# First turned weight tile of a two-layer LoRA kernel: loaded on ScalarE's queue, laid in two PSUM banks, copied by two engines

## The chip, the cores and the metric

The kernel runs on 1 core of one Trainium2 chip. The metric is device time in microseconds (us), the median of several runs. Engines are named as in the profile: PE is TensorE (PEld its weight loads), DVE is VectorE, ACT is ScalarE, POOL is GpSimd, SP is SyncE, which issues the transfers.

## The reference, cut to what matters

```python
# x: (8, 256, 1024) float32; W0, W1: (1024, 1024); ranks 32 and 16
def layer0(x, label, W, lora_A, lora_B_w):          # scale 0.5
    return x @ W.T + (x @ lora_A[label]) @ lora_B_w.T * 0.5
def layer1(x, slot, W, b, lora_As, lora_Bs):        # scale 2
    return x @ W.T + b + (x @ lora_As[slot]) @ lora_Bs[slot] * 2
x = x + layer0(x, itok_B_0_2, ...)                  # the label is chosen per batch
x = x + layer1(x, itok_B_0_23, ...)                 # and so is the slot
```

## The kernel before, in words

With the identity added to both weight matrices, the two layers are one product of x with V = (I + W0 transposed)(I + W1 transposed), and a low-rank part for each batch. The kernel first computes V once (up to about 89 us of the span), then goes over the 8 batches, each in some 22.6 us. Both products use a scheme of seven products of 512 x 512 quarters instead of eight. Every float32 operand is split in a high part (`_hi`, rounded to the matmul's format) and a low part (`_lo`, the rest); each product is hi x hi + hi x lo + lo x hi.

The order of the work is written out by hand for each engine; engines wait for each other by semaphores.

What matters here is the start, quarter (1,1) of both matrices: `a11` (of W0, loaded as it lies by `load_a`, 2 KB rows) and `b11` (of W1, which must be transposed first). Each comes in 4 tiles j = 0 to 3 of 256 KB. A tile of W1 is loaded to `n11` by `load_n` (in pieces of 512 bytes), the identity is added to its diagonal block (`n_eyed`; DVE does tile 0, POOL the others), PE transposes its four 128 x 128 blocks into one PSUM bank (`turn_b11`, semaphore `turned`), ACT copies the bank to `b11_hi` (`b11_high`, `w1_hi_made`), DVE computes `b11_lo` = bank - `b11_hi` (`b11_low`, `w1_lo_made`), and ACT copies the bank once more to `b11` (`b11_copy`, `w1_made`). For `a11`, DVE (tiles 0 and 1) casts to `a11_hi` (`w0_hi_made`); of tile 0 it casts columns 256 to 511 first, then adds the identity and casts columns 0 to 255.

PE starts with 14 matmuls on constants (`warm_up(14)`, 256 columns of bfloat16, whose result nothing reads), then transposes tile 0, issues 5 more such matmuls (`warm_up(5)`), and goes on with `vm1_high(0)`: 4 matmuls `a11_hi` x `b11_hi` (which wait for `w1_hi_made` and `w0_hi_made`), 4 with `b11_lo` (which wait for `w1_lo_made`), then the transposes of tile 1, and so on.

SP issues all transfers, in the order n11 tile 0, a11 tile 0, n11 tile 1, a11 tile 1, ... In the profile's rows `n`, `a`, `b_hi`, `a_hi`, `b_lo`, `a_lo`, `b` are these tiles with their numbers left out; `n_68` is n11, `a_49` is a11 and `b_52` is b11 in the listings of instructions.

Of the kernel before, what the change touches and what calls it, by code (L numbers as in the profile page):

```python
# [20 lines left out]
def two_layer_lora_kernel(nc, x, label0, slot1, w0, a0, b0w, w1, bias, a1, b1, out):  # L21
# [130 lines left out]
    with ExitStack() as ctx:  # L152
        bank = [ctx.enter_context(nc.psum_tensor(f"bank{n}", [P, 512], F32)) for n in range(8)]

        def sem(name):
            return ctx.enter_context(nc.semaphore(name))
# [64 lines left out]
        corr_done, h_made, u_hi_made, u_lo_made = sem("corr_done"), sem("h_made"), sem("u_hi_made"), sem("u_lo_made")  # L221
        e_st_made, m2_done = sem("e_st_made"), sem("m2_done")
        u0_hi_made, u0_lo_made = sem("u0_hi_made"), sem("u0_lo_made")
        m1_done, m6_done, m5_done, m7_done = sem("m1_done"), sem("m6_done"), sem("m5_done"), sem("m7_done")
        m1_made, u2_made, z_made, z2_made = sem("m1_made"), sem("u2_made"), sem("z_made"), sem("z2_made")
# [26 lines left out]
        def quarter(t, g):  # L252
            return t[:, HK * (g % 2):HK * (g % 2) + HK, P * (g // 2):P * (g // 2) + P]

        def last_half(h):
            dst = out[B - 1, :, sides[h]].rearrange("(p odd) i -> odd p i", odd=2)
            return dst[0], y[:, C11, sides[h]]
# [6 lines left out]
        def _(sp):  # L264
            w0_v = w0.rearrange("(b j p) (a i) -> p b j a i", b=2, p=P, a=2)
            w1_v = w1.rearrange("(n t p) (b j k) -> p n t b j k", n=2, p=P, b=2, k=P)

# [198 lines left out]
        def _(act):  # L466
# [188 lines left out]
            def batch(b, first, final):  # L655
# [60 lines left out]
        def _(dve):  # L716
# [23 lines left out]
            def b11_low(j):  # L740
                dve.wait_ge(w1_hi_made, j + 1)
                tt(b11_lo[:, j, :], TURN_BANK[j][:, :], b11_hi[:, j, :].bitcast(F32), ALU.subtract, w1_lo_made)
# [9 lines left out]
            def a11_high(j, cols):  # L752
                nc.vector.tensor_copy(a11_hi[:, j, cols], a11[:, j, cols]).then_inc(w0_hi_made, 1)

            for j in range(2):
                dve.wait_ge(a11_in[j], 16)
                if j == 0:
                    a11_high(0, sides[1])
                part = a11[:, j, P * j:P * j + P]
                tt(part, part, eye[:, :], ALU.add, w0_eyed)  # L760
                dve.wait_ge(w0_eyed, j + 1)
                a11_high(j, slice(0, H) if j else sides[0])
                b11_low(j)
                a11_low(j)
# [14 lines left out]
            def t1_sum(j):  # L779
                dve.wait_ge(w1_made, j + 1)  # L780
                tt(t1[:, j, :], TURN_BANK[T12_AT[j]][:, :], b11[:, j, :], ALU.subtract, t1_made)

            def t3_sum(j):
                dve.wait_ge(turned, T12_AT[j] + 1)
                dve.wait_ge(w1_made, HK + j + 1)
                tt(t3[:, j, :], TURN_BANK[T12_AT[j]][:, :], b22[:, j, :], ALU.subtract, t3_made)
# [63 lines left out]
            def b22_low(h):  # L850
                dve.wait_ge(w1_hi_made, 2 * HK + h + 1)
                dve.wait_ge(t2_made, h + 1)
                low(b22_lo, b22, b22_hi, PAIR[h], w1_lo_made)
# [7 lines left out]
            def t4_sum(h):  # L861

                dve.wait_ge(t2_made, h + 1)
                dve.wait_ge(w1_made, 2 * HK + 2 * h + 2)
                tt(t4[:, PAIR[h], :], b21[:, PAIR[h], :], t2[:, PAIR[h], :], ALU.subtract, t4_made)
# [32 lines left out]
            def b21_low(j):  # L898
                dve.wait_ge(w1_made, 2 * HK + j + 1)
                tt(b21_lo[:, j, :], TURN_BANK[T21_AT[j]][:, :], b21_hi[:, j, :].bitcast(F32), ALU.subtract, w1_lo_made)  # L900
# [205 lines left out]
            def batch(b, first, final):  # L1106
# [27 lines left out]
                def z_second():  # L1134
                    dve.wait_ge(m7_done, b + 1)
                    dve.wait_ge(z_made, b + 1)
                    tt(z_sum[:, :], BANK_D[:, :], z_sum[:, :], ALU.add, z2_made)
# [64 lines left out]
        def _(pe):  # L1202
# [8 lines left out]
            def row_tile(tile, j, m):  # L1211
                return tile[:, j, P * m:P * m + P]


            taken = ([(w1_made, j + 1) for j in range(HK)] + [(w1_made, HK + 1), (w1_made, HK + 2)]
                     + [(t1_made, 1), (t1_made, 2)] + [(w1_made, HK + 3), (w1_made, HK + 4)]
                     + [(t1_made, 3), (t1_made, 4)] + [(w1_lo_made, HK + 1)])

# [45 lines left out]
            def vm1_high(j):  # L1264

                pe.wait_ge(w1_hi_made, j + 1)
# [7 lines left out]
                pe.wait_ge(w1_lo_made, j + 1)  # L1274
                for m in range(HK):
                    mm(LOW[m][:, :], row_tile(a11_hi, j, m), b11_lo[:, j, :], False, False)
# [32 lines left out]
            pe.wait_ge(eye_steps, 2)  # L1309
            turn_b11(0)  # L1310
            warm_up(5)
# [47 lines left out]
            for j in range(HK):  # L1359
                pe.wait_ge(w1_lo_made, HK + j + 1)  # L1360
# [3 lines left out]
            pe.wait_ge(w1_made, 3 * HK)  # L1364
            c_first(0, A11)
# [6 lines left out]
            for j in range(HK):  # L1372
                q_step(Q_BANK[1], j, T3, j, j == 0, False)
            pe.wait_ge(w1_lo_made, 2 * HK + 2)
            for j in range(HK):
# [96 lines left out]
            def of(hi, lo):  # L1472
                return lambda k: (hi[:, k, :], lo[:, k, :])

            def batch(b, first, final):
# [33 lines left out]
                else:  # L1509
                    pe.wait_ge(c_made[C21], b)  # L1510
                product(BANK_D, s_of(3), of(vt3_hi, vt3_lo), True, m7_done)
                if not first:
# [14 lines left out]
                if not final:  # L1527
                    product(BANK_A, *second, False, m2_done, corrects=True)
# [70 lines left out]
```

## Time and profile before

| | |
|---|---|
| median of 3 runs | 294.64 us (294.39 to 294.78) |
| the profiled execution: its own time | 294.97 us |
| its span (first to last instruction) | 293.2 us |
| PE busy | 289.5 us (99%) |
| DVE / ACT / POOL busy | 242.9 / 153.6 / 31.3 us |

The span is shorter than the time of the same execution by 1.8 us, which lies around the kernel. The profile's busy time counts a matmul until its modelled end, so matmuls that follow each other overlap in the rows; how fast PE works is read from the distance of their starts.

### The profile page before, as it was taken

The page shows a single profiled execution, that of the slowest core. Times are in us where ns is not written, and L with a number is a line of the kernel's source. Part 1 is how long each engine was busy: PE and PEld are TensorE (multiplying, and loading weights), DVE is VectorE, ACT ScalarE, POOL GpSimd, SP SyncE. Part 2 cuts the span into 40 slices and gives each one's busy share as a digit, 9 for nine tenths or more (in the row PEclk, how much of TensorE's full clock was granted, in tenths as well). Part 3 has the DMA queues.
Part 4 walks back from the last instruction along what each step waited for, and adds up shares of the span by engine and source line. Part 5 has one row for each costly group of instructions (what it writes and reads, how often), then busy time and mean ns, then how long its engine had stood idle before and what let it go on. Part 6 is the DMA issues. An engine that isn't in the chain of part 4 may idle for free.

```text
span 293.2 us, 4450 instructions
## 1 busy us (share of the span) xinstructions
PE 289.5 (99%) x1337; PEld 236.1 (81%) x1337; DVE 242.9 (83%) x368; ACT 153.6 (52%) x270; POOL 31.3 (11%) x81
## 2 busy tenths in 40 slices
PE   8999999999999999999999999999999999999996
PEld 6888888888888888878878878878878878878875
DVE  3779998999999999999996897797798698695432
ACT  3574677879257637464453463373364355355120
POOL 0716500010000501000100100100100100100000
PEclk9999999999999999999999999999999999999999
DMA  6999530800006610074277077068068059013004
GB/s 200 315 275 345 79 43 6 141 1 2 0 0 110 97 28 1 6 125 157 46 117 199 22 120 198 18 101 221 6 108 212 15 101 233 6 36 144 0 1 145
DMA packets 100803, 29.17 MB, mean 99 GB/s; under 512 B 85548, under 2 KB 93996, under 8 KB 100788
## 3 DMA queue, kind: packets, MB, share of 16 engines
q1 hardware_dynamic: 100788, 28.99, 42.4%
q8 instruction: 7, 0.11, 0.2%
q14 instruction: 8, 0.07, 0.1%
HBM read 20.59 MB, written 8.39 MB: 99 GB/s over the span
## 4 chain that ended last, share of the span: by engine, by line
PE 99%; DVE 0%; issue 0%
PE bank L1204 95%; PE bank L1228 3%; PE bank L1449 1%; PE bank L1416 0%; DVE y L718 0%
## 5 line engine op out<-in xcount | busy, mean ns | idle before, releaser
L1204 PE MATMUL bank<-v_hi,lhs 128*128 128x512 f32 (+1 forms) x136 | 42.6, 378 | 0.0
L1204 PE MATMUL bank<-vt_lo,s_hi 128*128 128x512 f32 x96 | 37.4, 389 | 0.0
L1204 PE MATMUL bank<-vt_hi,s_hi 128*128 128x512 f32 x96 | 37.4, 389 | 0.0
L1204 PE MATMUL bank<-vt_hi,s_lo 128*128 128x512 f32 x96 | 37.4, 389 | 0.0
L969 DVE STREAM_TRANSPOSE xt<-raw 128x512 int32<-128x512 int32 x32 | 32.5, 1076 | 0.5 <-DMA raw<-in_x 0.4
L1204 PEld LDWEIGHTS bank<-v_hi,lhs 128*128 128x128 f32 x136 | 25.1, 188 | 4.8
L468 ACT ACTIVATE lhs<-xt 128x512 fp32r<-128x512 f32 x32 | 19.6, 626 | 13.0 <-PE bank L1204 12.7
L1204 PE MATMUL bank<-v_lo,lhs 128*128 128x512 f32 (+1 forms) x68 | 25.9, 380 | 0.0
L1204 PE MATMUL bank<-vt_hi,lhs 128*128 128x512 f32 x64 | 22.1, 406 | 0.0
L718 DVE TENSOR_TENSOR lhs<-xt,lhs 128x512 fp32r<-128x512 f32 x32 | 21.7, 687 | 0.3
L434 POOL CAST ac<-c_hi 128x128 fp32r (+1 forms) x16 | 7.1, 446 | 135.7 <-PE bank L1204 98.6
L718 DVE TENSOR_TENSOR s_lo<-s_sum,s_hi 128x512 fp32r<-128x512 f32 x32 | 21.2, 686 | 0.2 <-ACT s_hi L468 0.2
L1204 PEld LDWEIGHTS bank<-vt_lo,s_hi 128*128 128x128 f32 x96 | 18.0, 188 | 3.7
L1204 PEld LDWEIGHTS bank<-vt_hi,s_hi 128*128 128x128 f32 x96 | 18.0, 188 | 3.7
L1204 PEld LDWEIGHTS bank<-vt_hi,s_lo 128*128 128x128 f32 x96 | 18.0, 188 | 3.7
L468 ACT ACTIVATE s_hi<-s_sum 128x512 fp32r<-128x512 f32 x32 | 19.1, 624 | 2.1 <-DVE s_sum L718 1.8
L1204 PE MATMUL bank<-t_hi,s_hi 128*128 128x512 f32 x48 | 19.1, 397 | 0.0
L1204 PE MATMUL bank<-t_hi,s_lo 128*128 128x512 f32 x48 | 18.8, 391 | 0.0
L1204 PE MATMUL bank<-t_lo,s_hi 128*128 128x512 f32 x48 | 18.7, 390 | 0.0
L468 ACT ACTIVATE u_part<-bank 64x256 f32<-64x256 f32 x8 | 3.1, 381 | 28.0 <-PE bank L1204 28.0
L718 DVE TENSOR_TENSOR y<-bank,u_sum 128x512 f32<-128x512 f32 x16 | 11.0, 687 | 6.6 <-PE bank L1204 6.6
L468 ACT ACTIVATE vt_hi<-vt 128x512 fp32r<-128x512 f32 x16 | 10.1, 631 | 11.0 <-DVE vt L718 10.5
(167 smaller groups left out, 665.1 us busy)
## 6 DMA issues: line engine op xcount, KB each, us to landing
raw<-in_x SPq DMA_DIRECT2D x32, 256.0 KB, 4.8
out<-y SPq DMA_DIRECT2D x31, 256.0 KB, 2.7
n<-in_L_cond_W SPq DMA_DIRECT2D x16, 256.0 KB, 5.6
a<-in_L_cond_W SPq DMA_DIRECT2D x16, 256.0 KB, 5.6
a_raw<-in_L_cond_lora_A SPq DMA_DIRECT2D x8, 128.0 KB, 2.4
b_raw<-in_L_cond_lora_Bs SPq DMA_DIRECT2D x16, 64.0 KB, 2.2
e_raw<-in_L_cond_lora_Bs SPq DMA_DIRECT2D x32, 32.0 KB, 1.8
a_raw<-in_L_cond_lora_As SPq DMA_DIRECT2D x8, 64.0 KB, 2.6
```

Of the source, the lines that this page charges most:

```text
L434: nc.gpsimd.tensor_copy(ac[:, :, at_col:at_col + R1], c_hi[:, :, cols].bitcast(F32)).then_inc(ac_c_made, 1)
L468: nc.scalar.activation(out_ap, in_ap, COPY, scale=scale).then_inc(made, 1)
L718: nc.vector.tensor_tensor(out_ap, one, other, op).then_inc(made, 1)
L969: nc.vector.transpose(xt[:, n, :, :].rearrange("p e (s sb) -> p sb e s", sb=GR).bitcast(I32), rows[:, n // 2, n % 2].bitcast(I32)).then_in ...
L1204: return nc.tensor.matmul(ps, lhsT, rhs, start=start, stop=stop, skip_group_check=more)
L1228: last = nc.tensor.transpose(ps[:, P * t:P * t + P], tile[:, j, t, :], eye[:, :])
L1449: return nc.tensor.matmul(ps, e_st[rows, P * t:P * t + P], e_p[rows, cols], start=False, stop=True, skip_group_check=True, tile_position=( ...
```

## The change

Five edits.

1. n11 tile 0 is issued by ACT, as its first instruction, in place of SP. SP's list begins with a11 tile 0.
2. The four transposes of tile 0 go to two banks: blocks 2 and 3 to bank 4 (the bank of tile 2), blocks 1 and 0 to bank 6, in the order 2, 3, 1, 0. After block 3 a new semaphore `half_turned` is raised, after block 0 `turned` as before.
3. DVE casts columns 256 to 511 of `b11_hi` tile 0 from bank 4 after `half_turned`; ACT copies columns 0 to 255 from bank 6 after `turned`.
4. `b11_lo` and `b11` of tile 0 are made in two halves each (2 x 256 columns in place of 512), one for each bank.
5. The counts of `w1_hi_made`, `w1_lo_made` and `w1_made` are one higher from there on. `m2_done` and `m7_done` of the batches become one semaphore `m72_done`, raised twice per batch (odd counts in place of `m7_done`, even ones of `m2_done`). The transposes of tile 2 now wait for the copies of tile 0.

```diff
         TURN_BANK = [bank[n] for n in (6, 7, 4, 5, 6, 7, 4, 5, 6, 7, 4, 6, 7, 4, 6, 7)]
-        TURNED_THERE = {4: 0, 5: 1, 6: 2, 7: 3, 8: 4, 9: 5, 10: 6, 11: 8, 12: 9, 13: 10, 14: 11, 15: 12}
+        TURNED_THERE = {2: 0, 4: 0, 5: 1, 6: 2, 7: 3, 8: 4, 9: 5, 10: 6, 11: 8, 12: 9, 13: 10, 14: 11, 15: 12}
+        FIRST_BANK = [TURN_BANK[0], TURN_BANK[2]]
...
             for j in range(HK):
-                load_n(n11, 0, 0, j, n11_in[j])
+
+                if j > 0:
+                    load_n(n11, 0, 0, j, n11_in[j])
                 load_a(a11, 0, 0, j, a11_in[j])
...
             def b11_copy(j):
-                act.wait_ge(w1_lo_made, j + 1)
+                act.wait_ge(w1_lo_made, j + 2)
                 bank_copy(b11, j, TURN_BANK[j], w1_made)
 
-            for j in range(2):
-                b11_high(j)
-                b11_copy(j)
+            act.dma_start(n11[:, 0, :, :], w1_v[:, 0, :, 0, 0, :]).then_inc(n11_in[0], 16)
+            act.wait_ge(turned, 1)
+            copy(b11_hi[:, 0, sides[0]], FIRST_BANK[0][:, sides[0]], w1_hi_made)
+            for h in range(2):
+                act.wait_ge(w1_lo_made, h + 1)
+                copy(b11[:, 0, sides[h]], FIRST_BANK[h][:, sides[h]], w1_made)
+            b11_high(1)
+            b11_copy(1)
...
                 if not final:
-                    act.wait_ge(m2_done, b + 1)
+                    act.wait_ge(m72_done, 2 * b + 2)
                     a_high(b + 1, 1)
...
-                    act.wait_ge(m7_done, b + 1)
+                    act.wait_ge(m72_done, 2 * b + 1)
...
+            dve.wait_ge(half_turned, 1)
+            nc.vector.tensor_copy(b11_hi[:, 0, sides[1]], FIRST_BANK[1][:, sides[1]]).then_inc(w1_hi_made, 1)
             for j in range(2):
                 dve.wait_ge(a11_in[j], 16)
...
-                b11_low(j)
+                if j == 0:
+                    dve.wait_ge(w1_hi_made, 2)
+                    for h in range(2):
+                        tt(b11_lo[:, 0, sides[h]], FIRST_BANK[h][:, sides[h]], b11_hi[:, 0, sides[h]].bitcast(F32),
+                           ALU.subtract, w1_lo_made)
+                else:
+                    b11_low(j)
                 a11_low(j)
...
             warm_up(14)
             pe.wait_ge(eye_steps, 2)
-            turn_b11(0)
+
+            pe.wait_ge(n11_in[0], 16)
+            for t in (2, 3, 1, 0):
+                if t == 0:
+                    pe.wait_ge(n_eyed, 1)
+                last = nc.tensor.transpose(FIRST_BANK[t // 2][:, P * t:P * t + P], n11[:, 0, t, :], eye[:, :])
+                if t == 3:
+                    last.then_inc(half_turned, 1)
+            last.then_inc(turned, 1)
             warm_up(5)
             vm1_high(0)
             turn_b11(1)
```

ACT's first instructions, before the change (names as above; `turned` and the like are the semaphores that an instruction waits for):

```order
L465 UNCONDITIONAL_BRANCH [waits barrier_Pool_Activation_PE_DVE_SP_release]
L468 ACT_TABLE_LOAD
L468 ACTIVATE b_hi<-bank 128x512 [waits turned]
L468 ACTIVATE b_52<-bank 128x512 [waits w1_lo_made]
L468 ACTIVATE b_hi<-bank 128x512 [waits turned]
```

and the same place of the changed kernel:

```order
L470 UNCONDITIONAL_BRANCH [waits barrier_Pool_Activation_PE_DVE_SP_release]
L496 DMA n_68<-in_L_cond_W 128x4x128
L473 ACT_TABLE_LOAD
L473 ACTIVATE b_hi<-bank 128x256 [waits turned]
L473 ACTIVATE b_52<-bank 128x256 [waits w1_lo_made] x2
L473 ACTIVATE b_hi<-bank 128x512 [waits turned]
```

The transfer stands ahead of the table load, and the first two copies have become one of 256 columns and two of 256.

DVE's first instructions, before the change:

```order
L718 TENSOR_TENSOR n_68<-n_68,eye 128x128 [waits n11_in0,eye_steps]
L753 CAST a_hi<-a_49 128x256 [waits a11_in0]
L718 TENSOR_TENSOR a_49<-a_49,eye 128x128
L753 CAST a_hi<-a_49 128x256 [waits w0_eyed]
L718 TENSOR_TENSOR b_lo<-bank,b_hi 128x512 [waits w1_hi_made]
L718 TENSOR_TENSOR a_lo<-a_49,a_hi 128x512 [waits w0_hi_made]
```

and of the changed kernel:

```order
L728 TENSOR_TENSOR n_68<-n_68,eye 128x128 [waits n11_in0,eye_steps]
L766 CAST b_hi<-bank 128x256 [waits half_turned]
L763 CAST a_hi<-a_49 128x256 [waits a11_in0]
L728 TENSOR_TENSOR a_49<-a_49,eye 128x128
L763 CAST a_hi<-a_49 128x256 [waits w0_eyed]
L728 TENSOR_TENSOR b_lo<-bank,b_hi 128x256 [waits w1_hi_made]
L728 TENSOR_TENSOR b_lo<-bank,b_hi 128x256
L728 TENSOR_TENSOR a_lo<-a_49,a_hi 128x512 [waits w0_hi_made]
```

A cast from PSUM has come in ahead of the casts of a11, and the subtraction for `b_lo` is two. PE executes the same instructions as before in the same order; only the blocks and banks of its first four transposes differ.

## Rows read from the trace of the kernel before

**Rows 1.** The page: busy times, the chain that ended last.

```profile
span 293.2 us, 4450 instructions
PE 289.5 (99%) x1337; PEld 236.1 (81%) x1337; DVE 242.9 (83%) x368; ACT 153.6 (52%) x270; POOL 31.3 (11%) x81
...
PE 99%; DVE 0%; issue 0%
```

**Rows 2.** Windows: PE, PEld, DVE, ACT, POOL busy (count), PEclk, DMA share, GB/s.

```profile
9.16:24.00 14.84, 14.84 (x88) 12.79 (x87) 12.81 (x23) 10.44 (x19) 5.80 (x12) 1.00 1.02 299
24.00:60.00 36.00, 36.00 (x172) 30.09 (x171) 34.01 (x39) 24.96 (x36) 9.47 (x12) 1.00 0.54 104
60.00:285.00 225.00, 225.00 (x1010) 182.38 (x1009) 190.41 (x297) 115.14 (x213) 14.59 (x52) 1.00 0.36 79
```

**Rows 3.** Timeline from the start: start us, length us, engine, instruction.

```profile
0.78 0.45 SPq L272 DMA_DIRECT2D n<-in_L_cond_W  x1
0.79 1.28 ACT L468 ACT_TABLE_LOAD   x1 [0.79 <-PEq L1588]
...
0.83 3.15 PE L1204 MATMUL bank<-const-bfloat16-1.0 128*128 128x256 bf16 x14 [0.83 <-PEq L1588]
...
1.29 0.49 SPq L269 DMA_DIRECT2D a<-in_L_cond_W  x1
...
3.97 0.29 DVE L718 TENSOR_TENSOR n<-n,eye 128x128 f32<-128x128 f32 x1 [3.97 <-DMA n<-in_L_cond_W]
4.00 1.09 PE L1228 MATMUL bank<-eye,n 128*128 128x128 f32 x4
4.88 1.27 PE L1204 MATMUL bank<-const-bfloat16-1.0 128*128 128x256 bf16 x5
5.07 0.29 DVE L753 CAST a_hi<-a 128x256 fp32r<-128x256 f32 x1 [0.81 <-DMA a<-in_L_cond_W]
5.13 0.60 ACT L468 ACTIVATE b_hi<-bank 128x512 fp32r<-128x512 f32 x1 [3.06 <-PE bank L1228]
5.28 0.28 DVE L718 TENSOR_TENSOR a<-a,eye 128x128 f32<-128x128 f32 x1
...
5.59 0.29 DVE L753 CAST a_hi<-a 128x256 fp32r<-128x256 f32 x1
...
5.81 0.68 DVE L718 TENSOR_TENSOR b_lo<-bank,b_hi 128x512 fp32r<-128x512 f32 x1
...
6.41 0.68 DVE L718 TENSOR_TENSOR a_lo<-a,a_hi 128x512 fp32r<-128x512 f32 x1
6.75 0.87 PEld L1204 LDWEIGHTS bank<-b_lo,a_hi 128*128 128x128 f32 x4
6.97 1.07 PE L1204 MATMUL bank<-b_lo,a_hi 128*128 128x512 f32 x4
...
8.51 0.60 ACT L468 ACTIVATE b_hi<-bank 128x512 fp32r<-128x512 f32 x1 [1.39 <-PE bank L1228]
```

**Rows 4.** Timeline of the window 6.0 to 6.3: what runs in it.

```profile
5.74 0.42 PE L1204 MATMUL bank<-const-bfloat16-1.0 128*128 128x256 bf16 x1
5.78 0.69 PEld L1204 LDWEIGHTS bank<-b_hi,a_hi 128*128 128x128 f32 x3
...
5.81 0.86 PE L1204 MATMUL bank<-b_hi,a_hi 128*128 128x512 f32 x2
```

**Rows 5.** Tile views of n, then of a: time from issue to landing.

```profile
DMA to landing us min/median/max: 3.1/5.6/8.0
...
DMA to landing us min/median/max: 3.8/5.5/7.2
```

**Rows 6.** Page, costliest groups: xcount, busy us, mean ns, idle us before.

```profile
L1204 PE MATMUL bank<-vt_lo,s_hi 128*128 128x512 f32 x96 | 37.4, 389 | 0.0
...
L468 ACT ACTIVATE lhs<-xt 128x512 fp32r<-128x512 f32 x32 | 19.6, 626 | 13.0 <-PE bank L1204 12.7
...
L468 ACT ACTIVATE u_part<-bank 64x256 f32<-64x256 f32 x8 | 3.1, 381 | 28.0 <-PE bank L1204 28.0
```

More of the change, by code:

```diff
@@ L221, in two_layer_lora_kernel @@
         corr_done, h_made, u_hi_made, u_lo_made = sem("corr_done"), sem("h_made"), sem("u_hi_made"), sem("u_lo_made")
-        e_st_made, m2_done = sem("e_st_made"), sem("m2_done")
+        e_st_made, half_turned = sem("e_st_made"), sem("half_turned")
         u0_hi_made, u0_lo_made = sem("u0_hi_made"), sem("u0_lo_made")
-        m1_done, m6_done, m5_done, m7_done = sem("m1_done"), sem("m6_done"), sem("m5_done"), sem("m7_done")
+        m1_done, m6_done, m5_done, m72_done = sem("m1_done"), sem("m6_done"), sem("m5_done"), sem("m72_done")
         m1_made, u2_made, z_made, z2_made = sem("m1_made"), sem("u2_made"), sem("z_made"), sem("z2_made")
@@ L253, in quarter @@
             return t[:, HK * (g % 2):HK * (g % 2) + HK, P * (g // 2):P * (g // 2) + P]
+        w1_v = w1.rearrange("(n t p) (b j k) -> p n t b j k", n=2, p=P, b=2, k=P)
         def last_half(h):
@@ L265, in _ @@
             w0_v = w0.rearrange("(b j p) (a i) -> p b j a i", b=2, p=P, a=2)
-            w1_v = w1.rearrange("(n t p) (b j k) -> p n t b j k", n=2, p=P, b=2, k=P)
             def load_a(tile, a, b, j, there):
@@ L740, in b11_low @@
             def b11_low(j):
-                dve.wait_ge(w1_hi_made, j + 1)
+                dve.wait_ge(w1_hi_made, j + 2)
                 tt(b11_lo[:, j, :], TURN_BANK[j][:, :], b11_hi[:, j, :].bitcast(F32), ALU.subtract, w1_lo_made)
@@ L779, in t1_sum @@
             def t1_sum(j):
-                dve.wait_ge(w1_made, j + 1)
+                dve.wait_ge(w1_made, j + 2)
                 tt(t1[:, j, :], TURN_BANK[T12_AT[j]][:, :], b11[:, j, :], ALU.subtract, t1_made)
@@ L784, in t3_sum @@
                 dve.wait_ge(turned, T12_AT[j] + 1)
-                dve.wait_ge(w1_made, HK + j + 1)
+                dve.wait_ge(w1_made, HK + j + 2)
                 tt(t3[:, j, :], TURN_BANK[T12_AT[j]][:, :], b22[:, j, :], ALU.subtract, t3_made)
@@ L850, in b22_low @@
             def b22_low(h):
-                dve.wait_ge(w1_hi_made, 2 * HK + h + 1)
+                dve.wait_ge(w1_hi_made, 2 * HK + h + 2)
                 dve.wait_ge(t2_made, h + 1)
@@ L863, in t4_sum @@
                 dve.wait_ge(t2_made, h + 1)
-                dve.wait_ge(w1_made, 2 * HK + 2 * h + 2)
+                dve.wait_ge(w1_made, 2 * HK + 2 * h + 3)
                 tt(t4[:, PAIR[h], :], b21[:, PAIR[h], :], t2[:, PAIR[h], :], ALU.subtract, t4_made)
@@ L898, in b21_low @@
             def b21_low(j):
-                dve.wait_ge(w1_made, 2 * HK + j + 1)
+                dve.wait_ge(w1_made, 2 * HK + j + 2)
                 tt(b21_lo[:, j, :], TURN_BANK[T21_AT[j]][:, :], b21_hi[:, j, :].bitcast(F32), ALU.subtract, w1_lo_made)
@@ L1134, in z_second @@
                 def z_second():
-                    dve.wait_ge(m7_done, b + 1)
+                    dve.wait_ge(m72_done, 2 * b + 1)
                     dve.wait_ge(z_made, b + 1)
@@ L1212, in row_tile @@
                 return tile[:, j, P * m:P * m + P]
-            taken = ([(w1_made, j + 1) for j in range(HK)] + [(w1_made, HK + 1), (w1_made, HK + 2)]
-                     + [(t1_made, 1), (t1_made, 2)] + [(w1_made, HK + 3), (w1_made, HK + 4)]
-                     + [(t1_made, 3), (t1_made, 4)] + [(w1_lo_made, HK + 1)])
+            taken = ([(w1_made, j + 2) for j in range(HK)] + [(w1_made, HK + 2), (w1_made, HK + 3)]
+                     + [(t1_made, 1), (t1_made, 2)] + [(w1_made, HK + 4), (w1_made, HK + 5)]
+                     + [(t1_made, 3), (t1_made, 4)] + [(w1_lo_made, HK + 2)])
             def turn(tile, j, n, eyed=0):
@@ L1264, in vm1_high @@
             def vm1_high(j):
-                pe.wait_ge(w1_hi_made, j + 1)
+                pe.wait_ge(w1_hi_made, j + 2)
                 if j > 0:
@@ L1273, in vm1_high @@
                     mm(LOW[m][:, :], row_tile(a11_hi, j, m), b11_hi[:, j, :], j == 0, False)
-                pe.wait_ge(w1_lo_made, j + 1)
+                pe.wait_ge(w1_lo_made, j + 2)
                 for m in range(HK):
@@ L1359, in _ @@
             for j in range(HK):
-                pe.wait_ge(w1_lo_made, HK + j + 1)
+                pe.wait_ge(w1_lo_made, HK + j + 2)
                 last = q_step(Q_BANK[0], HK + j, B21, j, False, j == HK - 1)
@@ L1363, in _ @@
             pe.wait_ge(a1_lo_made, 1)
-            pe.wait_ge(w1_made, 3 * HK)
+            pe.wait_ge(w1_made, 3 * HK + 1)
             c_first(0, A11)
@@ L1373, in _ @@
                 q_step(Q_BANK[1], j, T3, j, j == 0, False)
-            pe.wait_ge(w1_lo_made, 2 * HK + 2)
+            pe.wait_ge(w1_lo_made, 2 * HK + 3)
             for j in range(HK):
@@ L1510, in batch @@
                     pe.wait_ge(c_made[C21], b)
-                product(BANK_D, s_of(3), of(vt3_hi, vt3_lo), True, m7_done)
+                product(BANK_D, s_of(3), of(vt3_hi, vt3_lo), True, m72_done)
                 if not first:
@@ L1527, in batch @@
                 if not final:
-                    product(BANK_A, *second, False, m2_done, corrects=True)
+                    product(BANK_A, *second, False, m72_done, corrects=True)
                     h_ready()
```

## The prediction

> **What bounds the kernel now.** I read the page first: PE is busy 289.5 of 293.2 us and the chain that ended last is PE alone for 99% of the span [rows 1]. The windows say where the rest is: from 9.16 us to 285 us PE is busy in every hundredth of a us [rows 2]. So nothing after the first ten microseconds waits for data, and whatever the change does there must show as a shift of everything behind: the kernel ends earlier or later by as much as PE's first real matmuls do, and by nothing else. The timeline of the start is the place to read [rows 3].
>
> There PE does this. It works on constants from 0.83 us; n11 tile 0 has landed when DVE and PE go on at 3.97 and 4.00; four transposes; five matmuls on constants; then the first matmul of the product at 5.81 [rows 4], those with b_lo at 6.97 [rows 3]. Two candidates could hold that 5.81. One is the copy of ACT, 5.13 to 5.73, with the weight load at 5.78 [rows 3, 4]. The other is PE itself. The 14 matmuls on constants take 3.15 us with the last one 0.42 long: 2.73 over 13 distances, 0.21 us for 256 columns, which is 1.2 GHz, the lower level of the clock. The last of the five starts at 5.74 [rows 4], so its columns occupy the array until 5.74 + 0.21 = 5.95. The first real matmul then has to fall in from 5.95, whatever its row says as a start. The second real one agrees: two of them take 0.86 us from 5.81 [rows 4], and one at full clock is 0.39 long [rows 6], so it starts at 6.28. That is 0.33 behind 5.95, midway between 0.43 (512 columns at 1.2 GHz) and 0.23 (the distance at 2.4 GHz, (1.07 - 0.39) / 3 [rows 3, 6]). So half of its columns ran at either level, and the clock rose near 6.15. The clock column of the windows shows 1.00 throughout and doesn't tell this; the distances do.
>
> So both are nearly tied: ACT's copy lets the array start near 5.95 too (weight load at 5.78, and some 0.1 to 0.2 until its matmul runs), and the five matmuls on constants end there. The start of the transposes, which is the landing of n11 tile 0, sets both: 4.00 plus 9 distances of 0.21 is 5.92, plus a rest of 0.03.
>
> **The change part by part.**
>
> *Half copies of b11_hi.* ACT copied 512 columns in 0.60 us [rows 3]; a copy of 256 columns took 0.38 [rows 6]. It ends 0.22 earlier, at 5.51 instead of 5.73 if the landing is the same. DVE's cast from the other bank can start when the second transpose is through, 0.7 us behind the start of the first (0.21 distance, 0.42 length, a wait's 0.04), at T + 0.7, where T is the start of the transposes. I take 0.3 for it (256 columns from SBUF took 0.29 [rows 3]; this one reads PSUM, which no row has for a cast; the far bound is half of the 0.68 subtraction and a fixed part, 0.45). It ends by T + 1.15 at the latest, ahead of ACT. So b11_hi is ready 0.22 earlier. What this gives on PE is at most 0.03, since the matmuls on constants stand until T + 1.95 while the clock is at the lower level. The gain of 0.22 is covered; it would be had in full only if the clock rose before the transposes.
>
> *b_lo.* DVE's row is now: cast b_hi, cast a_hi, add, cast a_hi, two halves of b_lo. With distances from the rows (5.07 to 5.28 to 5.59 to 5.81: 0.21, 0.31, 0.22; a 512-column subtraction frees DVE after 0.60, 5.81 to 6.41; half of it about 0.33) b_lo is complete at T + 0.71 + 0.24 + 0.74 + 0.33 + 0.41 = T + 2.43; before it was 6.49 = T + 2.49 [rows 3]. The additional cast is paid by the fact that a11 no longer is waited for: the cast of a_hi began at 5.07 because a11 landed then. Equal, so no gain, and no loss as long as a11 is there by T + 0.95.
>
> *The second copy, b11, in halves.* 2 x 0.38 in place of 0.60 on ACT, which next has work when tile 1 is turned, at 8.51 [rows 3]. Covered.
>
> *The semaphore `m72_done`.* The counts keep the same two waits. In the loop over batches ACT gets two more register instructions per round; ACT waits 12.7 us in all in front of one group of copies there and PE is busy all through [rows 2, 6]. Zero.
>
> *The transfers.* This is the term that decides. Before, SP issued n11 tile 0 at 0.78 and a11 tile 0 at 1.29 [rows 3]; they landed 3.1 and 3.8 later, 3.9 and 5.1 [rows 3, 5]. ACT left the same barrier at 0.79 [rows 3], so n11 tile 0 is issued no earlier than before. What changes is the company: a11 tile 0 is issued at 0.78 too, on the other queue, and takes part in the same 16 DMA engines from the beginning instead of half a microsecond later and behind. a11 and all that SP issues behind it go 0.5 us earlier; n11 tile 0, on which everything hangs, can only lose. Bounds: nothing lost (landing 3.9, T = 4.00), and a11's bytes wholly ahead (n11 lands last, at the old 5.0 to 5.1 of a11, T = 5.1). A tile of 256 KB takes 0.87 us at the 299 GB/s of a stretch in which the DMA engines are busy throughout [rows 2]; of a11's 0.87 us the part counts that is moved in front of n11's last pieces. With two queues served in turn I take half of it, 0.45: T = 4.45.
>
> [...]
>
> *What 0.45 later costs PE.* Until 6.15 the array works at half speed, so a delay there is partly paid back: fewer columns run at 1.2 GHz. From T = 4.45 eight of the nine distances pass by 6.15 (1.70 us), the ninth at 2.4 GHz takes 0.11: 6.26. The first real matmul takes 0.23 more; the second runs from 6.49 where it was 6.28. That is +0.21. b_lo is ready at 4.45 + 2.43 = 6.88, its weight load would stand at about 6.95: just not late. Behind it the order on PE is unchanged, and SP's transfers come earlier, so the shift stays +0.21 to the end.
>
> **Sum.** 0.21 from the landing, -0.03 to 0 from the half copies, 0 from the others: about +0.2 us. Against the profiled execution that is 294.97 + 0.2 = 295.2; that execution lies 0.33 above the median, and I give the median: 294.64 + 0.2 = 294.8. A measurement of this kernel tells about 0.2% (0.6 us) from no change, so the forecast is "no difference".
>
> **The rivals.**
>
> *a11 goes ahead of n11 (slower).* With T = 5.1, ACT's half copy ends at 5.1 + 1.09 + 0.04 + 0.38 = 6.6, b_lo at 5.1 + 2.43 = 7.5, and the matmuls with b_lo start at 7.75 (0.22 behind their weight load) instead of 6.97: +0.8 us, 295.4. [...] Against: n11's issue takes less time (0.45 against 0.49), so it is not behind. Chance 0.12. Above T = 4.85 it decides at the 0.6 us bound.
>
> *The clock rises later (slower).* The clock rose at 6.15 after work with one break of 0.2 us before 4.00. At T = 4.45 the break is 0.7 us. If it puts off the rise, each us of that costs half a us of matmuls at 1.2 GHz; I price a rise at 9.2, three groups of matmuls and one of transposes later: 3.0 / 2 = 1.5 us, 296.1. For it: the order of events alone; one rise is all that the trace shows. [...] Against: the break stays short beside the work around it. Chance 0.07.
>
> *No contention (slightly faster).* n11 lands as before or, alone in its queue, a little earlier. PE could start at 3.77, when its last warm-up leaves the array (it starts at 3.98 - 0.42 = 3.56 and needs 0.21). Then nine distances end at 5.7, the first real matmul runs mostly at 1.2 GHz and is through at about 6.12, the second at 6.35 instead of 6.51: -0.16 us, 294.5. Even this is within 0.2%. A gain of 0.6 us has no place in the rows: b_lo at T + 2.43 would allow at most 0.3. Chance 0.2, and 0.05 beyond for a faster result that I can't name.
>
> **How the numbers follow.** The forecast (+0.0 to +0.6) has 0.56, no contention 0.20, a11 ahead 0.12, the clock 0.07, unnamed gain 0.05. Of a11 ahead about two thirds lie over 0.6 us. Faster by over 0.2%: 0.05; slower: 0.08 + 0.07, 0.15; within: 0.80. The range goes from no contention with the spread of the runs (-0.25) to 294.2, and up to a11 ahead, 295.4; the late clock and a small rest are left out.
>
> **What would show it.** n11's transfer on ACT's queue and DVE's add of the identity later than 3.97, near 4.4; the cast of b_hi by DVE 0.7 behind the first transpose; ACT's copy of 256 columns about 0.38; a11's cast waiting for no DMA; the second real matmul near 6.5; PE busy from there as before. Wrong if DVE's add stands at 3.97 or earlier while the time falls by 0.6 (then ACT's copy was the bound after all), or if matmuls of 512 columns keep the long form beyond 6.5 (the clock).

## The result: 0.6% slower

The changed kernel takes 296.89 us (median of 9 runs, 296.00 to 297.46) against 294.92 us for the kernel before (9 runs, 294.39 to 295.89). The medians are 1.97 us apart. The ratio is 1.0063, with a 95% interval from 1.0052 to 1.0074, which is 1.9 us (1.5 to 2.2): slower by 0.6%, where "no difference" was forecast. The range, 294.2 to 295.4, doesn't hold it. The profiled execution took 297.46 us with a span of 295.7, 2.5 us more than the span of before, so it is one of the longer ones.

The timeline of the changed kernel's start (start us, length us, engine, instruction; ACTq and SPq are issues of transfers):

```profile
0.78 0.40 SPq L272 DMA_DIRECT2D a<-in_L_cond_W  x1
0.78 0.47 ACTq L496 DMA_DIRECT2D n<-in_L_cond_W  x1
...
0.83 3.15 PE L1222 MATMUL bank<-const-bfloat16-1.0 128*128 128x256 bf16 x14 [0.83 <-PEq L1614]
...
5.34 0.29 DVE L728 TENSOR_TENSOR n<-n,eye 128x128 f32<-128x128 f32 x1 [5.34 <-DMA n<-in_L_cond_W]
...
5.38 1.09 PE L1333 MATMUL bank<-eye,n 128*128 128x128 f32 x4 [1.40 <-DMA n<-in_L_cond_W]
...
6.08 0.42 DVE L766 CAST b_hi<-bank 128x256 fp32r<-128x256 f32 x1 [0.44 <-PE bank L1333]
...
6.42 0.35 DVE L763 CAST a_hi<-a 128x256 fp32r<-128x256 f32 x1
6.50 0.38 ACT L473 ACTIVATE b_hi<-bank 128x256 fp32r<-128x256 f32 x1 [3.93 <-PE bank L1333]
...
7.18 2.06 PE L1222 MATMUL bank<-b_hi,a_hi 128*128 128x512 f32 x4
7.21 0.74 DVE L728 TENSOR_TENSOR b_lo<-bank,b_hi 128x256 fp32r<-128x256 f32 x2
...
9.04 1.51 PE L1222 MATMUL bank<-b_lo,a_hi 128*128 128x512 f32 x4
...
11.02 0.60 ACT L473 ACTIVATE b_hi<-bank 128x512 fp32r<-128x512 f32 x1 [2.65 <-PE bank L1246]
```

Two things have happened. First, n11 tile 0 landed 1.37 us later: DVE's add stands at 5.34 where it stood at 3.97 [rows 3]. PE's row of the transposes says that it was idle for 1.40 us before them, waiting for this transfer. Second, the matmuls behind run longer than before. Taken one by one in the trace, the four with b_hi start at 7.18, 7.76, 8.18 and 8.61 and the first three with b_lo at 9.04, 9.46 and 9.89: from the second one on they are 0.43 apart, the pace of the matmuls on constants in front of them (256 columns every 0.213 us), where in the kernel before they were 0.23 apart from the second one on. Only the last distance, 9.89 to 10.16, is shorter, so the clock rose near 10 us. The trace says the same: beside the instructions it has entries of the granted clock, and the first of them, a share of 1.00, begins at 9.94 us here and at 6.15 in the kernel before. The four with b_lo begin 2.07 late (9.04 against 6.97), and ACT's copy of tile 1 is 2.51 late (11.02 against 8.51). The spans differ by 2.5, so that is the whole difference, and the windows say that nothing is added behind it (busy us of PE, PEld, DVE, ACT, POOL, clock, DMA share, GB/s):

```profile
5.00:24.00 19.00, 18.62 (x96) 15.64 (x97) 15.23 (x31) 10.63 (x20) 8.29 (x14) 1.00 1.13 325
24.00:285.00 261.00, 261.00 (x1181) 212.72 (x1180) 225.71 (x335) 140.88 (x250) 20.41 (x62) 1.00 0.38 81
```

PE is busy 261.00 of 261.00 us, as in [rows 2]; its only idle time behind 5.00 is the 0.38 us in front of the transposes. The chain of waits of the changed kernel has the transfer in it, 2% of the span, which it had not before [rows 1]:

```profile
PE 97%; DMA 2%; DVE 0%; issue 0%
PE bank L1222 93%; PE bank L1246 2%; DMA n<-in_L_cond_W 2%; PE bank L1475 1%; PE bank L1333 0%; PE bank L1442 0%; DVE y L728 0%
```

### The profile page after: what moved, and what is told of

The parts are those of the page before. It is cut to its first block, busy times and chain, and to the rows that moved or that the text cites. A ratio compares the mean times of both kernels' runs of the same rounds, so it can differ in the third digit from the quotient of the medians.

```text
span 295.7 us, 4466 instructions
## 1 busy us (share of the span) xinstructions
PE 290.6 (98%) x1337; PEld 236.9 (80%) x1337; DVE 243.8 (82%) x370; ACT 153.6 (52%) x271; POOL 29.4 (10%) x81
## 4 chain that ended last, share of the span: by engine, by line
PE 97%; DMA 2%; DVE 0%; issue 0%
PE bank L1222 93%; PE bank L1246 2%; DMA n<-in_L_cond_W 2%; PE bank L1475 1%; PE bank L1333 0%; PE bank L1442 0%; DVE y L728 0%
## 5 line engine op out<-in xcount | busy, mean ns | idle before, releaser
L1222 PE MATMUL bank<-lhs,ac 128*128 128x512 f32 x64 | 15.8, 389 | 0.0
```

What stands on the lines that cost most here:

```text
L1222: return nc.tensor.matmul(ps, lhsT, rhs, start=start, stop=stop, skip_group_check=more)
```

## The experiments

All times are medians, each against runs of the kernel before made beside it. Of each kernel one execution was profiled; of the others only the times are known. The questions: is it the queue or the half copies; why does n11 come so late; and what does the clock add?

### The queue alone, the half copies alone

First the queue alone, on the kernel before:

```diff
+            act.dma_start(n11[:, 0, :, :], w1_v[:, 0, :, 0, 0, :]).then_inc(n11_in[0], 16)
             for j in range(2):
                 b11_high(j)
...
-                load_n(n11, 0, 0, j, n11_in[j])
+                if j > 0:
+                    load_n(n11, 0, 0, j, n11_in[j])
```

> The kernel before, with nothing changed but that n11 tile 0 is issued by ScalarE in place of SyncE. Theory 1 (the two queues share the DMA engines, and the late landing moves all that follows): n11 tile 0 lands at about 5.3 us as in the changed kernel (before: 3.9), and the time is 2 to 2.5 us above the kernel before. Theory 2 (the late landing or the loss comes from the half copies and their waits): landing at 3.9 and no loss.

296.80 us against 295.05, ratio 1.0052 (1.0035 to 1.0070). The transfer landed at 5.26. The loss is there without one half copy, and with 5 runs it can't be told from that of the whole change (1.0052 to 1.0074).

Then the changed kernel with the transfer back on SyncE:

```diff
-            act.dma_start(n11[:, 0, :, :], w1_v[:, 0, :, 0, 0, :]).then_inc(n11_in[0], 16)
...
-                if j > 0:
-                    load_n(n11, 0, 0, j, n11_in[j])
+                load_n(n11, 0, 0, j, n11_in[j])
```

> The changed kernel with n11 tile 0 issued by SyncE first, as before; the two banks, the half copies and the merged semaphore stay. Theory 1: landing at 3.9 again, b_hi ready at 5.5 instead of 5.73, hidden behind the matmuls on constants: within 0.3 us of the kernel before. Theory 2 (half copies cost): 1 to 2.5 us slower. Theory 3 (the clock hides nothing): 0.2 us faster.

295.09 us against 295.05, ratio 1.0004 (0.9995 to 1.0013). With the landing in time, the two banks, the half copies and the merged semaphore neither cost nor give anything that can be measured. The timeline of this run shows how the shorter copy is lost:

```profile
4.29 1.08 PE L1330 MATMUL bank<-eye,n 128*128 128x128 f32 x4 [0.32 <-DMA n<-in_L_cond_W]
5.17 1.27 PE L1219 MATMUL bank<-const-bfloat16-1.0 128*128 128x256 bf16 x5
...
5.41 0.38 ACT L471 ACTIVATE b_hi<-bank 128x256 fp32r<-128x256 f32 x1 [3.35 <-PE bank L1330]
...
6.10 1.29 PE L1219 MATMUL bank<-b_hi,a_hi 128*128 128x512 f32 x4
```

ACT was through at 5.79, but the real matmuls start at 6.10, 1.81 behind the transposes, as before (4.00 and 5.81): the matmuls on constants fill that time. The landing was 0.3 later in this execution (4.26 against 3.97), though SyncE's list was that of the kernel before; this much it varies by itself.

### Why n11 is late: which transfer goes first

Queue for queue, the transfers of the changed kernel from 1.8 to 2.8 us and, behind the "...", from 2.8 to 3.8 (packets, MB, share of the 16 engines). q1 is SyncE's queue, q10 ScalarE's:

```profile
q1 hardware_dynamic: 79, 0.16, 75.1%
...
q10 hardware_dynamic: 259, 0.13, 44.6%
q1 hardware_dynamic: 61, 0.10, 41.0%
```

In the first microsecond in which bytes move, ScalarE's queue moves nothing at all. The 79 packets carry 0.16 MB, 2 KB each: rows of a11. It isn't a sharing in turn, as I had assumed. Either ScalarE's queue starts late in itself, or something lets a11 pass first. The next kernels tell these apart. Each is the kernel before with one tile, or half of one, issued by ScalarE; their diffs leave out lines already shown.

With the queues changed about (a11 on ScalarE, n11 first on SyncE):

```diff
+            act.dma_start(a11[:, 0, :], w0_v[:, 0, 0, 0, :]).then_inc(a11_in[0], 16)
...
-                load_a(a11, 0, 0, j, a11_in[j])
+                if j > 0:
+                    load_a(a11, 0, 0, j, a11_in[j])
```

> The kernel before with a11 tile 0 issued by ScalarE at 0.8 us and n11 tile 0 still first on SyncE. Two transfers start together as in the changed kernel, with the queues changed about. Theory A (the engines serve the two queues in turn, and the tile in 512-byte pieces loses): n11 tile 0 lands late again, 4.6 to 5.3 us. Theory B (a transfer issued by ScalarE starts behind the one that SyncE issued, whatever it holds): n11 tile 0 lands near 3.9 as before and a11 tile 0 is the late one, 5.0 or later. Time: A 1 to 2 us slower, B within 0.6 us.

296.18 us against 295.07, ratio 1.0042 (1.0024 to 1.0059). Its queues in the same two stretches:

```profile
q10 hardware_dynamic: 72, 0.15, 57.5%
...
q1 hardware_dynamic: 294, 0.15, 50.4%
q10 hardware_dynamic: 69, 0.11, 35.3%
```

Now SyncE's queue is the one that moves nothing for a microsecond, and n11 on it landed at 5.16. Theory B, by which ScalarE's transfer stands behind, is refuted; the landing is as theory A said, but not for its reason. The ten times lie in two groups, five from 295.57 to 295.64 and five from 296.71 to 297.55; the section on the clock comes back to them. The timeline from 0.7 to 1.2 us gives the two issues:

```profile
0.78 0.46 SPq L273 DMA_DIRECT2D n<-in_L_cond_W  x1
0.79 0.42 ACTq L493 DMA_DIRECT2D a<-in_L_cond_W  x1
```

a11's issue ended at 1.21 and n11's at 1.24; in the changed kernel they ended at 1.18 and 1.25, and in the kernel with the queue alone at 1.18 and 1.26. Each time a11's ended first, and a11 went first.

With ScalarE's transfer alone (n11 on ScalarE, and SyncE waiting for its landing):

```diff
+            sp.wait_ge(n11_in[0], 16)
             for j in range(HK):
```

> n11 tile 0 issued by ScalarE at 0.8 us, and SyncE issues nothing before it has landed. For its landing only: everything behind is late and the time says nothing. Theory B1 (a transfer on ScalarE's queue starts a microsecond late in itself): landing at 4.8 or later though nothing else moves. Theory B2 (it starts late because SyncE's transfer is prepared first): landing at 3.9.

The landing, by DVE's add:

```profile
0.78 0.43 ACTq L494 DMA_DIRECT2D n<-in_L_cond_W  x1
...
3.73 0.29 DVE L722 TENSOR_TENSOR n<-n,eye 128x128 f32<-128x128 f32 x1 [3.73 <-DMA n<-in_L_cond_W]
```

Landed by 3.73: the queue isn't slow. (Its time, 297.79 us from one run, says nothing here, for its other loads wait.)

With n11 on ScalarE again and SyncE's a11 put back to about where it was in time (1.49, before the change 1.29), behind the two small index loads:

```diff
+            sp.dma_start(index[0:1, 0:B], label0.rearrange("(o b) -> o b", o=1)).then_inc(index_in, 16)
+            sp.dma_start(index[0:1, B:2 * B], slot1.rearrange("(o b) -> o b", o=1)).then_inc(index_in, 16)
             for j in range(HK):
...
-                if j == 2:
-                    sp.dma_start(index[0:1, 0:B], label0.rearrange("(o b) -> o b", o=1)).then_inc(index_in, 16)
-                    sp.dma_start(index[0:1, B:2 * B], slot1.rearrange("(o b) -> o b", o=1)).then_inc(index_in, 16)
```

> n11 tile 0 issued by ScalarE at 0.8 us; SyncE issues the two small index transfers first and then a11 tile 0 at about 1.4 us, where it stood before the change. Theory B2 (who is first is prepared first): n11 tile 0 lands near 3.9 to 4.2 and the time is within 0.6 us of the kernel before. Theory A (served in turn): landing at 4.5 or later. Theory B1 (ScalarE's queue starts late in itself): 4.9 or later, 1 to 2.5 us slower.

294.88 us against 295.07, ratio 0.9990 (0.9978 to 1.0002). The loss is gone:

```profile
0.79 0.43 ACTq L492 DMA_DIRECT2D n<-in_L_cond_W  x1
...
1.49 0.36 SPq L270 DMA_DIRECT2D a<-in_L_cond_W  x1
...
3.75 0.29 DVE L720 TENSOR_TENSOR n<-n,eye 128x128 f32<-128x128 f32 x1 [3.75 <-DMA n<-in_L_cond_W]
...
4.51 0.29 DVE L755 CAST a_hi<-a 128x256 fp32r<-128x256 f32 x1 [0.47 <-DMA a<-in_L_cond_W]
```

Its queues from 1.8 to 2.8 us: only ScalarE's moves, now 400 packets of n11.

```profile
q10 hardware_dynamic: 400, 0.20, 69.1%
```

With one index load instead of two ahead of it, so that a11's issue starts 0.3 us earlier:

```diff
+            sp.dma_start(index[0:1, 0:B], label0.rearrange("(o b) -> o b", o=1)).then_inc(index_in, 16)
             for j in range(HK):
```

> The kernel before; ScalarE issues n11 tile 0, SyncE issues one small index transfer and then a11 tile 0, at about 1.2 us, so that its issue ends 0.3 us behind that of n11 (in the changed kernel it ended 0.07 us ahead). Theory B2 (whoever has issued first is prepared first, whatever it holds): n11 lands at 3.6 to 3.9 and a11 by 4.5; time within 0.4 us of the kernel before. Rival (the tile in 2 KB rows goes ahead of the one in 512-byte pieces when both are near in time): n11 at 4.5 or later, 1 us slower or more.

295.19 us against 294.97, ratio 1.0001 (0.9991 to 1.0012).

```profile
0.79 0.43 ACTq L493 DMA_DIRECT2D n<-in_L_cond_W  x1
1.21 0.37 SPq L270 DMA_DIRECT2D a<-in_L_cond_W  x1
...
3.87 0.29 DVE L721 TENSOR_TENSOR n<-n,eye 128x128 f32<-128x128 f32 x1 [3.87 <-DMA n<-in_L_cond_W]
```

n11's issue ended at 1.22 and a11's at 1.58, and n11 went first. And the mirror, on the kernel before: ScalarE issues the two index loads and then a11, SyncE n11 first.

> The kernel before; ScalarE issues the two index transfers and then a11 tile 0, at about 1.5 us; SyncE issues n11 tile 0 first. The mirror of the run in which ScalarE had n11 and SyncE came later. If only the order in time counts and not the queue: n11 lands by 3.9, a11 near 4.5, the time within 0.5 us of the kernel before. If ScalarE's queue goes ahead of SyncE's or takes turns with it: n11 at 4.3 or later, 0.5 us and more slower.

295.65 us against 295.09, ratio 1.0028 (1.0009 to 1.0046). n11 was there at 3.97, as before. But a11, whose issue ended at 1.95, behind that of SyncE's second tile of n11 (1.79), was cast only at 5.54, and PE waited 0.78 us for it, in an execution in which the clock was already high. So the order held, my figure for a11 (4.5) did not, and it cost 0.6 us.

```profile
1.58 0.37 ACTq L492 DMA_DIRECT2D a<-in_L_cond_W  x1
...
3.97 0.29 DVE L720 TENSOR_TENSOR n<-n,eye 128x128 f32<-128x128 f32 x1 [3.97 <-DMA n<-in_L_cond_W]
5.54 0.29 DVE L755 CAST a_hi<-a 128x256 fp32r<-128x256 f32 x1 [1.28 <-DMA a<-in_L_cond_W]
5.98 1.29 PE L1206 MATMUL bank<-b_hi,a_hi 128*128 128x512 f32 x4 [0.78 <-DVE a_hi L755]
```

Last, n11 tile 0 as two transfers of 128 KB, one on each queue:

```diff
+                    sp.dma_start(n11[:, 0, 0:2, :], w1_v[:, 0, 0:2, 0, 0, :]).then_inc(n11_in[0], 16)
...
+            act.dma_start(n11[:, 0, 2:4, :], w1_v[:, 0, 2:4, 0, 0, :]).then_inc(n11_in[0], 16)
...
-            dve.wait_ge(n11_in[0], 16)
+            dve.wait_ge(n11_in[0], 32)
```

> The kernel before with n11 tile 0 as two transfers of 128 KB, blocks 0 and 1 issued by SyncE first, blocks 2 and 3 by ScalarE at the same time. If the preparation of a transfer is what takes time and goes on for both queues at once, the tile lands near 3.5 us and the transposes start at about 3.8, 0.2 us earlier: time 0 to 0.2 us below the kernel before. Theory B: the half on ScalarE's queue starts late and a11 stands ahead of it, so the tile lands at 4.5 or later: 0.6 to 1.5 us slower.

294.89 us against 295.07, ratio 0.9995 (0.9981 to 1.0008). Both queues move in the first microsecond (237 packets on q1, 115 on q10; in the trace the first ones on q10 come between 2.2 and 2.3, on q1 between 1.8 and 1.9), DVE's add stands at 3.78 and the transposes start at 3.82; no measurable gain.

All of it fits one order: in each of these kernels n11 tile 0 and a11 tile 0 began to move in the order in which their issues ended, whichever queue they were on. Behind a tile of 256 KB the other tile's first bytes came 0.9 to 1.1 us later (n11's at 2.89 behind a11's at 1.81 in the changed kernel, a11's at 2.83 behind n11's at 1.97 with one index load ahead), behind the half tile 0.3 (2.21 against 1.88). Once both moved, they shared the 16 DMA engines: from 2.8 to 4.8 in the changed kernel q1's packets took 55.5% of the engines' time and q10's 44.1%. From 3.8 to 4.8 q10 (n11) had 269 packets and q1, already at later tiles, 378. So n11 in second place lost twice: it started about a microsecond later, and it took about 2.5 us from its first bytes to the landing (2.89 to 5.34), where with nothing else moving it took 1.8 (1.90 to 3.73). What remains inferred is the order at a distance of 0.03 to 0.08 us: in all four kernels in which the issues ran side by side (the changed kernel, with the gap filled, the queue alone, the queues changed about) a11's ended first and went first. No run took the lead from it at that distance, so a rule by which its 2 KB rows win a near tie isn't excluded; a lead of 0.36 us for n11 overrules it. Nor is a11's issue the shorter one as such: it took 0.40 and 0.42 side by side with n11's 0.47 and 0.46, but 0.49 against 0.45 in the kernel before, where it stood second [rows 3].

### The clock

Seven more matmuls on constants in the changed kernel, so that PE has no break before the late landing:

```diff
-            warm_up(14)
+            warm_up(21)
```

> The changed kernel with warm_up(21) in place of warm_up(14): 7 more matmuls on constants of 0.21 us each, so that TensorE has hardly a break before the late landing at 5.3. Theory 1 (the break put off the rise of the clock): the clock rises near 6.2 again, the 128x512 matmuls behind are 0.23 apart at once, and the time is 1.2 to 1.5 us below the changed kernel, still about 1 us above the kernel before. Theory 2 (the clock rises when it does, by chance): long matmuls until about 9.9 as in the changed kernel, no gain.

296.04 us (295.94 to 296.15, 7 runs) against 295.05, ratio 1.0032 (1.0021 to 1.0043). The landing is nearly as late as in the changed kernel (5.17 against 5.34), and the time is 0.85 below it, less than the 1.2 to 1.5 that I expected.

```profile
0.83 4.45 PE L1222 MATMUL bank<-const-bfloat16-1.0 128*128 128x256 bf16 x21 [0.83 <-PEq L1614]
5.21 0.64 PE L1333 MATMUL bank<-eye,n 128*128 128x128 f32 x4
...
6.42 1.43 PE L1222 MATMUL bank<-b_hi,a_hi 128*128 128x512 f32 x4
...
7.12 0.30 PEld L1222 LDWEIGHTS bank<-b_hi,a_hi 128*128 128x128 f32 x2 [0.43 <-DVE a_hi L763]
...
7.78 0.76 PEld L1222 LDWEIGHTS bank<-b_lo,a_hi 128*128 128x128 f32 x4 [0.37 <-DVE b_lo L728]
7.78 1.19 PE L1222 MATMUL bank<-b_lo,a_hi 128*128 128x512 f32 x4
```

The four transposes take 0.64 where they took 1.09: the clock was high at 5.21 already (the trace's first entry begins at 4.95), earlier than the 6.2 that I expected, and stays so. 1.0 us over the kernel before is left. It is not the landing alone. The weight loads waited 0.43 us for the second cast of a_hi and 0.37 for b_lo: in DVE's row the cast of b_hi stands ahead of those of a11, and the add to a11 took 0.54 us here, where elsewhere it took 0.28. The kernel with the queues changed about has no such cast; in its profiled execution, too, the landing was late (5.16) and the clock high:

```profile
5.20 0.64 PE L1231 MATMUL bank<-eye,n 128*128 128x128 f32 x4 [1.22 <-DMA n<-in_L_cond_W]
...
7.55 1.09 PE L1207 MATMUL bank<-b_lo,a_hi 128*128 128x512 f32 x4
```

Its b_lo matmuls start 0.58 later than in the kernel before (6.97) and its time was 295.57, 0.5 over the kernel before; in the kernel with the gap filled they start 0.81 later. So of the 1.0 about 0.5 is the landing; the rest goes with the edits beside the queue. That rest rests on two profiled executions and on times: all seven with the gap filled lie from 295.94 to 296.15, the lower five with the queues changed about from 295.57 to 295.64.

The reverse, a break in the kernel before with nothing landing later:

```diff
-            warm_up(14)
+            warm_up(7)
```

> The kernel before with warm_up(7) in place of warm_up(14): TensorE idles from about 2.3 to 4.0 us, nothing else changes. Theory 1 (a break puts off the rise): matmuls stay 0.43 apart until some us later than 6.2, and the time is 1 to 1.7 us above the kernel before although no data come later. Theory 2 (chance): no difference beyond the spread.

296.73 us (295.25 to 297.94) against 295.05, ratio 1.0051 (1.0031 to 1.0071).

```profile
3.85 1.09 PE L1228 MATMUL bank<-eye,n 128*128 128x128 f32 x4 [1.37 <-DMA n<-in_L_cond_W]
...
5.66 2.05 PE L1204 MATMUL bank<-b_hi,a_hi 128*128 128x512 f32 x4
7.51 1.91 PE L1204 MATMUL bank<-b_lo,a_hi 128*128 128x512 f32 x4
9.22 0.63 PE L1228 MATMUL bank<-eye,n 128*128 128x128 f32 x4
```

n11 landed at 3.82, earlier than in the kernel before, and still the eight real matmuls run 0.43 apart up to 9.2 (the trace's first entry of the clock begins at 9.28). The break of 1.4 us alone costs 1.7 us in the median. It also spreads the times: 2.7 us between the fastest and the slowest of 9 runs, 0.9 in the 24 runs of the kernel before beside it.

A break didn't put off the rise every time, though. With the queues changed about PE had a break of 1.22 us before the transposes, and in the profiled execution they still ran at the high clock (0.64 us, the first entry at 4.06). The times say the same: every kernel with a break and a late landing has a lower group and, 0.6 us and more above it, an upper one (changed kernel 3 of 9 runs at 296.0 to 296.1 and 6 from 296.71; queue alone 1 of 5 at 295.64; queues changed about 5 of 10). That the lower group is the early rise is seen in one profile and inferred for the rest.

### The whole change with the order put right

> The changed kernel whole, but SyncE issues the two small index transfers ahead of a11 tile 0, which it so issues at about 1.4 us. If the loss of the change is only that a11's transfer was prepared ahead of n11's, n11 lands near 3.7 and all of the loss (2 us) is gone: within 0.5 us of the kernel before, like the same edit without half copies. If halves, waits or the merged semaphore cost something of their own, 0.5 to 1 us stay.

295.18 us against 295.09, ratio 0.9999 (0.9990 to 1.0008): the changed kernel with the two index loads ahead of a11 loses nothing. Beside it the same with 3 matmuls on constants for 5 behind the transposes (`warm_up(3)`):

> As the run beside it, with warm_up(3) in place of warm_up(5) behind the first transposes. Theory of the prediction (the matmuls on constants cover the shorter copy): TensorE's first real matmul starts 0.2 to 0.3 us earlier than beside it, at 1.2 GHz, for about 0.1 us in all. Rival (the copy or the casts hold it): no earlier start, and an idle stretch in front of it.

295.21 us against 295.09, ratio 1.0003 (0.9993 to 1.0013). The time is the same, and the gain of 0.1 us that the prediction's theory gives would be too small to see. In both profiled executions the clock rose early (transposes in 0.77 and 0.64 us, first entries at 4.29 and 4.13), so they don't answer the question about the lower level. What they show is what waits next when the constants are through: the casts of a11. First the kernel with 5 constants:

```profile
4.79 0.39 ACT L472 ACTIVATE b_hi<-bank 128x256 fp32r<-128x256 f32 x1 [2.26 <-PE bank L1332]
...
5.72 0.29 DVE L762 CAST a_hi<-a 128x256 fp32r<-128x256 f32 x1 [0.72 <-DMA a<-in_L_cond_W]
...
6.16 1.17 PE L1221 MATMUL bank<-b_hi,a_hi 128*128 128x512 f32 x4 [0.85 <-DVE a_hi L762]
```

The same kernel with 3 constants:

```profile
4.93 0.28 DVE L762 CAST a_hi<-a 128x256 fp32r<-128x256 f32 x1
5.36 1.17 PE L1221 MATMUL bank<-b_hi,a_hi 128*128 128x512 f32 x4 [0.24 <-DVE a_hi L762]
```

In the first b_hi was ready at 5.18 and PE idled 0.85 us for a_hi, whose tile had landed late. In the second PE idled 0.24 us though a11 was there: the cast of a_hi waited for nothing but DVE itself, which had the cast of b_hi (4.59) ahead of it. So the half copies were covered from both sides: with the rise at 6.35 (the first entry in the run of the half copies alone) by the matmuls on constants (real matmuls at 6.10, ACT through at 5.79), with the early ones by a11's landing or by DVE's own row.

## Why the prediction was wrong

**What bounds the kernel: right.** Everything behind the first eleven microseconds kept its length, and PE was busy all through it; the whole difference is the later start of the real matmuls and the slower pace of the first eight.

**The half copies, b_lo, the second copy, `m72_done`: right.** Forecast -0.03 to 0; measured 1.0004 (0.9995 to 1.0013) for all of them together. DVE's cast of 256 columns from PSUM took 0.42 us (I took 0.3, bound 0.45), ACT's copy of 256 columns 0.38 as taken. Two remarks beside the term don't hold. That the gain of 0.22 "would be had in full" with an early clock: with 3 constants and the clock high b_hi was ready at 5.20 and PE started at 5.36, held by DVE. And that the additional cast costs DVE nothing doesn't hold where a11 landed ahead of n11: there, with the clock high, b_lo's matmuls stood 0.23 later than without that cast (7.78 against 7.55, one execution each).

**The transfers: this step failed.** The prediction put n11's loss at half of a11's 0.87 us, "with two queues served in turn I take half of it, 0.45: T = 4.45", and bounded it by T = 5.1. T was 5.38. That a11 takes part in the 16 DMA engines from the beginning is what happened: from 1.8 to 2.8 q1's packets took 75.1% of their time. But the turns, and the half that follows from them, were an assumption that no run shows: n11's first packet came at 2.89, 1.08 behind a11's at 1.81, and only then did both queues move, with 55.5% and 44.1% of the engines' time from 2.8 to 4.8. What stands in the place of the 0.45 is a landing 1.37 later. The upper bound failed as well, for I took a11's old landing at 5.1 as the end of both, while n11 in second place took 4.5 us from issue to landing, against the 3.1 of [rows 5]. Worked with the measured T by the prediction's own rule (b_lo at T + 2.43, its matmuls 0.25 behind) b_lo's matmuls would start at 8.06, +1.1 us. In the kernel with the gap filled, where the clock was high in time, T was 5.21: the rule gives 7.89, the trace shows 7.78, and the median is +1.0. So the path from landing to PE was right, and its input wrong. Two premises led there. "n11's issue takes less time (0.45 against 0.49), so it is not behind" took the lengths from a row in which a11's issue stood second; side by side a11's was the shorter and ended first. And the part of a11 that counts was sized by 0.87 us at 299 GB/s, where in the first microsecond its queue moved 0.16 MB, 162 GB/s. (The bound "above T = 4.85" comes out at 4.92 by the terms beside it, 6.97 + 0.6 - 2.43 - 0.22; nothing hangs on it.)

**The clock: right mechanism, wrong chance.** The 1.2 GHz of the prediction is 256 columns in 0.213 us, 1.20 columns a ns; the 2.4 GHz is its double and an estimate, for the traces hold a share and no frequency. With the clock high, matmuls on constants stood 0.111 apart (gap filled, 5.68 to 6.13), 2.3 columns a ns, and real ones of 512 columns 0.227 (b_lo's in the kernel before), 2.26 columns a ns. The rival priced a late rise at +1.5 us on top and gave it 0.07, because the break was "short beside the work around it". The break became 1.4 us by the first error, and the two rivals, taken as alternatives, came together. By medians 1.0 us is there with the gap filled and 0.85 more without, 1.85 in all, of the 1.9 (the two sets have their own runs of the kernel before, 295.05 and 294.92). In the profiled execution the clock's part was larger: of 2.51, 1.37 is the landing in the start of the first real matmul, and 1.14 came on top of it in the eight matmuls behind, up to a rise near 10 where the rival had priced 9.2. The parts aren't simple sums: a break alone, without any late data, cost 1.7 us (1.0051), and the lower times with the queues changed about say 0.5 for a late landing alone. That a break puts off the rise is shown by the times (0.2 us of spread with the gap filled, 24 runs of the kernel before within 0.9, 8 of 9 with a break above all of them); why some executions with a break escape it is open.

**"Even this is within 0.2%."** The order put right gives 0.9990 (0.9978 to 1.0002), and split over both queues 0.9995: the gain of 0.16 that the rival without contention was given fits, but neither is told from no difference, and two more kernels with n11 first on ScalarE's queue show none of it (1.0001 and 0.9999). No version here beats the kernel before.

## What to carry to other kernels

Here, moving a first load to another engine's queue saved nothing for that load and let the other queue's load overtake it; if one must move, make sure that its issue ends first, by ordering something small ahead of the competitor, and read the landing from the first instruction that uses it. Matmuls on constants that reached up to the late data kept all seven times within 0.2 us (295.94 to 296.15), while a break of 1.4 us in the kernel before left 8 of 9 times above all 24 without it: whoever lets the data come later should lengthen them, and must count the late landing and the late clock together. The shorter copy was worth nothing here (1.0004), for filler work or the other operand covered it, so look for both before making one. And the cast put first in DVE's row delayed what stood behind it when its own data came late: b_lo's matmuls by 0.23 us.

## What the runs showed of the hardware

- Two tiles of 256 KB issued at the same 0.78 us from two engines: for the first microsecond in which bytes moved, one queue had all the packets (79 to 0, 72 to 0 with the queues changed about), and the second tile landed 4.3 to 4.5 us behind its issue where it took 3.1 in first place.
- The clock's rise differed from one execution to another. Read from the distances of matmuls, it came near 6.15 us in the kernel before, near 8.6 with the queue alone, near 9.3 in the kernel before with a break and near 10 in the changed kernel, but before 5.3 us in five others, whose landings were early or late (gap filled, queues changed about, the mirror, both kernels with halves and the order put right), by their transposes of 0.64 to 0.77 us. The first entries of the granted clock in the traces begin at 6.15, 8.58, 9.28 and 9.94 us, and in the five others at 4.95, 4.06, 3.50, 4.29 (5 constants) and 4.13 (3 constants); the trace with one index load ahead has none. The mirror's PE had the same work as that of the kernel before up to 3.8 us, and its 14 constants took 2.98 us against 3.15: there the clock rose before they ended. With a break the kernel before spread over 2.7 us, without one over 0.9, and with the gap filled the changed kernel over 0.2.
- Before its first entry the clock column of the profile showed 1.00, also in stretches in which 512-column matmuls were 0.43 us apart; there the distances told. It showed the other level once PE's work was over: 0.50 from 292.9 to 293.1 us in the kernel before. Matmuls on constants (256 columns) stood 0.213 us apart before the first entry and 0.111 after it (gap filled).
